# Rotary products by VectorE straight from the PSUM bank, sums by POOL, and one output addition moved up in an attention, LoRA and expert kernel

## The chip, the cores and the metric

The kernel runs on one core of a Trainium2 chip. The core has five engines with a queue of instructions each: TensorE (PE, matrix products into the eight PSUM banks), VectorE (DVE), ScalarE (ACT), GpSimd (POOL) and SyncE (SP, which issues DMAs). They run side by side and wait for each other through semaphores. The metric is the device time of one execution in microseconds, lower is better.

## The reference, cut to what matters

`x` has 64 batches of 64 tokens with 512 channels. The attention block is the part that the change touches:

```
h = cond(x) @ WA + bA;  kv_lat, q_lat = split(h)            # 2 x 128 latents per token
kRt = rope(h @ WB + bB);  qRt = rope(h @ WC + bC)            # one rotary key (64), 16 rotary queries (64 each)
rope(y) = y * cos + rot(y) * sin,   rot(y) = (-y1, y0, -y3, y2, ...)
scores = (q . k + qRt . kRt) * scale, causal;  attn = softmax(scores)
x = x + (attn @ v) @ WZ + bZ
x = x + ffn(cond2(x))                                        # LoRA product, then top-2 routing to 4 experts
```

`cos` and `sin` depend on the position and on the pair of features; both features of a pair have the same angle.

## The kernel before

Weights are first multiplied together (`absorb_weights`): the query weights into the key weights (`Ah`, `Al`), the value weights into WZ (`Mh`, `Ml`). An fp32 product is made of three matmuls on a high and a low part (`split_product`, L93). Then comes `attention`, then `routing`, then `experts`. `routing` and `experts` are not touched.

`attention` goes over 8 groups of 8 batches, so 512 token columns (GT) per group. Within a group there are 8 steps `i` (4 pairs of batches, times 2 halves of the 16 heads): scores, softmax, transpose of the probabilities, `mix` with the values, and `wz`, the output product of that step, which is accumulated in the single bank `bank_o` over eight heads and added to `x_res` by VectorE (`x2_tile`, L726). The next step's `wz` may not start before that addition (wait on `x2_ev`, L957).

The projections of a group are: one for the rotary keys (`rope_keys`, six matmuls into `bank_p1`), eight for the rotary queries (`q_rope_mm`, steps u = 0 to 7, two heads each, six matmuls), and 16 key heads (`keys_absorbed`, three matmuls). They share two banks, `bank_p0` and `bank_p1`: the query steps 0 to 3 use bank 0 and the key heads 0 to 3 bank 1; the key heads 4 and up, and the query steps 4 to 7, use the two by turns.

Every engine's order is written out by hand. TensorE's program at the boundary from group g to g+1 (L1031 to L1045) is: the first four heads of `wz` step 5, the rotary keys, then for u = 0 to 3 query step u, key head u and one more head of `wz` step 5; then the key heads 4 to 7, `wz` step 6 (whose first matmul waits for `x2_tile` of step 5), and the scores of g+1. In the middle of a group (L991 to L1002) the query steps 4 to 7 are interleaved with `wz` step 0, and after a transpose the key heads 8 and 9 follow, then `mix` and `wz` step 1 interleaved with the other key heads. In the first group, before the loop, the projections stand without output products between them.

What happens to a rotary projection before the change, with r counting keys and query steps:

- ScalarE (`keys_raw` L528, `q_raw` L534) copies the bank with its bias into `rope_raw` and raises `raw_ev`. This releases the bank: `q_rope_mm` and `keys_absorbed` on TensorE wait for `raw_ev` (L878, L886, L890, L892).
- POOL (`keys_cos` L447, `q_cos` L454) multiplies `rope_raw` by the cosine table into `k_rope` or `q_rope`.
- VectorE (`turn` L664) swaps neighbouring partitions of `rope_raw` with a shuffle, multiplies the result by the signed sine table, and adds it to POOL's product (`keys_rope` L677, `queries_rope` L685). This raises `rope_done`, for which the scores wait (L905).

VectorE's program at the boundary (L803 to L817) is: the low part of `mix` step 6, the rotary keys, the query steps 0 to 3, `x2_tile` step 5, `x2_tile` step 6, and the softmax of the next group. In the middle (L761 to L770): the query steps 4 and 5, a softmax sum, query step 6, `x2_tile` step 0, query step 7.

Of the kernel before, what the change touches and what calls it, by code (L numbers as in the profile page):

```python
# [63 lines left out]
def const_columns():  # L64
    def rope(feature, size):
        theta = np.exp(-(feature // 2).astype(np.float32) / np.float32(size)
                       * np.log(np.float32(10000.0))).astype(np.float32)
        angle = (np.arange(1, C + 1, dtype=np.float32)[None] * theta[:, None]).astype(np.float32)
        sign = np.where(feature % 2 == 0, -1.0, 1.0).astype(np.float32)[:, None]
        return np.cos(angle), np.sin(angle) * sign  # L70
# [264 lines left out]
def attention(nc, K, A, W, out):  # L335

    with ExitStack() as ctx:
# [6 lines left out]
        def sem(name):  # L344
# [15 lines left out]
        q_rope = sb("q_rope", [P, UB, GT])  # L360
        raw, swapped = sb("rope_raw", [P, 2, GT]), sb("rope_swapped", [P, GT])
        lat_bias = (raw[:, 0, :], swapped)
        bias_sel = nc.alloc_sbuf_tensor_at("bias_sel", [2 * LOW, GB, C], F32R, offset=nc.sbuf_base - GT * 4)
        score = sb("score", [P, HB, C])
# [13 lines left out]
        names = """xres_biased wrap_ev bias_sel_ready bias_mm lb_ev cond_mm cond_hi cond_lo lat_mm lat_ev lat_hi lat_lo  # L378
            kvt_mm kvt_ev keys_mm qr_mm raw_ev swap_ev cos_ev sin_ev rope_done ka_mm ka_ev s_mm score_ev max_ev sub_ev
            exp_ev sum_ev inv_ev prob_ev pt_mm pt_ev mix0_mm mix1_mm mix0_hi mix1_hi mix0_lo mix1_lo wz_mm x2_ev""".split()  # L380
# [58 lines left out]
        def _(pool):  # L439
# [6 lines left out]

            def keys_cos(g):  # L447
                pool.wait_ge(S["raw_ev"], g * NR + 1)
                nc.gpsimd.tensor_tensor(k_rope[:, :].rearrange("p (b t) -> p b t", b=GB),
                                        raw[:, 0, :].rearrange("p (b t) -> p b t", b=GB),  # L450
                                        K.parts["cosk"].unsqueeze(1).to_broadcast([P, GB, C]),
                                        ALU.mult).then_inc(S["cos_ev"], 1)

            def q_cos(g, u):  # L454
                pool.wait_ge(S["raw_ev"], g * NR + u + 2)
                cos = K.parts["cosq"][:, u * C:(u + 1) * C]
                nc.gpsimd.tensor_tensor(q_rope[:, u % UB, :].rearrange("p (b t) -> p b t", b=GB),  # L457
                                        raw[:, (u + 1) % 2, :].rearrange("p (b t) -> p b t", b=GB),
                                        cos.unsqueeze(1).to_broadcast([P, GB, C]), ALU.mult).then_inc(S["cos_ev"], 1)


# [11 lines left out]
            def project_front(g):  # L473
                keys_cos(g)
                for u in range(UB):
                    q_cos(g, u)

# [6 lines left out]
            def body(g, more):  # L484
                gated(g, 2)
                residual_bias(g, 0)
                for u in range(UB, NU):
                    q_cos(g, u)
                gated(g, 3)
# [17 lines left out]
        def _(act):  # L507
# [19 lines left out]

            def keys_raw(g):  # L528
                act.wait_ge(S["lat_ev"], g * 2 + 2)
                act.wait_ge(S["keys_mm"], g + 1)  # L530
                nc.scalar.activation(raw[:, 0, :], bank_p[1][:, :], ACT.Identity, bias=K["bB"][:, 0:1]
                                     ).then_inc(S["raw_ev"], 1)

            def q_raw(g, u):  # L534
                act.wait_ge(S["qr_mm"], g * NU + u + 1)
                if u:
                    act.wait_ge(S["swap_ev"], g * NR + u)
                    act.wait_ge(S["cos_ev"], g * NR + u)
                nc.scalar.activation(raw[:, (u + 1) % 2, :], bank_p[q_bank(u)][:, :], ACT.Identity, bias=K["bC"][:, u:u + 1]  # L539
                                     ).then_inc(S["raw_ev"], 1)  # L540

            def keys_absorbed(g, h):
# [19 lines left out]
            def first():  # L562
                latent_bias(0)
                for c in range(TC):
                    cond_hi(0, c)
                latent_hi(0, 0)
                latent_hi(0, 1)
                keys_raw(0)
                for u in range(UB):
                    q_raw(0, u)  # L570
                    keys_absorbed(0, u)
                for h in range(UB, HB):
                    keys_absorbed(0, h)
                exps(0, 0)
                kv_tokens(0, 0)
                kv_tokens(0, 1)
                exps(0, 1)

            def body(g, more):
# [5 lines left out]
                mix_hi(g, 1)  # L585
                q_raw(g, UB)
                exps(g, 3)
                for u in range(UB + 1, NU):
                    q_raw(g, u)

# [32 lines left out]
                if more:  # L623
                    keys_raw(g + 1)
                    for u in range(UB):
                        q_raw(g + 1, u)
                        keys_absorbed(g + 1, u)
# [14 lines left out]
        def _(dve):  # L642
# [20 lines left out]

            def turn(r, k, sin):  # L664

                dve.wait_ge(S["raw_ev"], r + 1)
                dve.wait_ge(S["rope_done"], r)
                nc.vector.memset(wait_here[:, :], 0.0)
                nc.vector.stream_shuffle(swapped[:, :], raw[:, k, :], [i ^ 1 for i in range(32)]
                                         ).then_inc(S["swap_ev"], 1)  # L670
                dve.wait_ge(S["swap_ev"], r + 1)
                v = swapped[:, :].rearrange("p (b t) -> p b t", b=GB)
                nc.vector.tensor_tensor(v, v, sin.unsqueeze(1).to_broadcast([P, GB, C]), ALU.mult
                                        ).then_inc(S["sin_ev"], 1)
                dve.wait_ge(S["sin_ev"], r + 1)

            def keys_rope(g):  # L677
                r = g * NR
                dve.wait_ge(S["lat_ev"], g * 2 + 2)
                turn(r, 0, K.parts["sink"])  # L680
                dve.wait_ge(S["cos_ev"], r + 1)
                nc.vector.tensor_tensor(k_rope[:, :], k_rope[:, :], swapped[:, :], ALU.add
                                        ).then_inc(S["rope_done"], 1)

            def queries_rope(g, u):  # L685
                r = g * NR + 1 + u
                turn(r, (u + 1) % 2, K.parts["sinq"][:, u * C:(u + 1) * C])
                dve.wait_ge(S["cos_ev"], r + 1)
                nc.vector.tensor_tensor(q_rope[:, u % UB, :], q_rope[:, u % UB, :], swapped[:, :], ALU.add
                                        ).then_inc(S["rope_done"], 1)  # L690

# [64 lines left out]
            def body(g, more):  # L756
# [1384 lines left out]
```

## Time and profile before

| | us |
|---|---|
| median of the two runs | 1875.18 (1873.96 to 1876.39) |
| the profiled execution, its time | 1876.52 |
| its span, first to last instruction | 1874.7 |
| TensorE busy | 1797.6 (96%) |
| VectorE busy | 925.5 (49%) |
| POOL busy | 702.7 (37%) |
| ScalarE busy | 630.2 (34%) |

Engines are PE, PEld (weight load of TensorE), DVE, ACT, POOL and SP. L12 is line 12 of the kernel. In a list of waits a row reads: who waited, at which tile and line, for whom; us in total, times, longest. In a timeline a row has the start and the duration in us, the engine, the line, the operation and its output and input tiles; in brackets stands the idle time before it and what ended it. Ends of matmuls are modelled, so that successive ones overlap: their spacing is the difference of their starts. PEclk is the granted TensorE clock as a share of full speed.

### The profile page before, as it was taken

What the parts mean: (1) busy time and instruction counts of PE and PEld (TensorE: products, weight loads), DVE (VectorE), ACT (ScalarE), POOL (GpSimd) and SP (SyncE); (2) the same over time, 40 slices, a digit from 0 to 9 for tenths busy, and PEclk for the clock granted to TensorE, in tenths of its full rate; (3) what the DMA queues carried; (4) which work ended last, traced back from release to release, by engine and by line L of the source; (5) the groups of instructions that cost most, each with busy time, mean ns of one, the idle gap of its engine ahead of it and who ended that gap; (6) DMA issues with size and microseconds to landing.
All of it is one profiled execution on the core that took longest, in us unless ns stands there. A gap on an engine that the chain in (4) does not pass through costs nothing. (4 is left out here: it accounts for less than half of the span.)

```text
span 1874.7 us, 29070 instructions
## 1 busy us (share of the span) xinstructions
PE 1797.6 (96%) x10656; PEld 1425.3 (76%) x10656; DVE 925.5 (49%) x1579; ACT 630.2 (34%) x1092; POOL 702.7 (37%) x526
## 2 busy tenths in 40 slices
PE   6799999999999999999999997999999999999997
PEld 4577777777777777777787776888888888888886
DVE  3565767566566656656423683242424233333332
ACT  4333333333333333333223112333333333333332
POOL 1231323123132312313000034565757575757564
PEclk9999999999999999999999998999999999999999
DMA  7000102010010102002123115033304230522011
GB/s 265 23 1 23 46 7 62 7 61 3 29 40 6 63 7 63 1 29 51 45 96 113 56 68 191 23 79 111 78 0 112 90 67 0 134 90 45 0 23 23
DMA packets 68795, 104.49 MB, mean 56 GB/s; under 512 B 12528, under 2 KB 29680, under 8 KB 68720
## 3 DMA queue, kind: packets, MB, share of 16 engines
q1 hardware_dynamic: 53568, 76.85, 12.3%
q0 software_dynamic: 7200, 16.78, 5.0%
q10 hardware_dynamic: 7952, 9.73, 1.4%
q8 instruction: 62, 1.02, 0.2%
q14 instruction: 13, 0.11, 0.0%
HBM read 78.18 MB, written 25.17 MB: 55 GB/s over the span
## 5 line engine op out<-in xcount | busy, mean ns | idle before, releaser
L1911 DVE CAST hh<-hid 128x512 fp32r<-128x512 f32 x128 | 95.5, 746 | 437.5 <-ACT hid L1838 437.5
L1754 POOL TENSOR_TENSOR w1l<-w_raw,w1h 128x512 fp32r<-128x512 f32 x112 | 185.0, 1652 | 146.7 <-ACT w1h L1830 146.6
L464 POOL TENSOR_TENSOR prob<-prob,rinv 128x512 f32<-128x512 f32 x64 | 66.7, 1043 | 436.2 <-DVE rinv L724 436.2
L97 PE MATMUL bank_o<-Mh,mix_h 128*128 128x512 f32 x512 | 210.2, 411 | 17.9 <-DVE x_res L731 16.5
L97 PE MATMUL e_h<-xh,w1h 128*128 (+1 forms) x512 | 201.0, 393 | 5.9 <-POOL w1l L1754 5.9
L99 PE MATMUL bank_o<-Mh,mix_l 128*128 128x512 f32 x512 | 203.6, 398 | 0.0
L98 PE MATMUL bank_o<-Ml,mix_h 128*128 128x512 f32 x512 | 203.5, 398 | 0.0
L97 PE MATMUL e_y<-w2h,hh 128*128 128x512 f32 x512 | 200.8, 392 | 1.5 <-DVE hl L1913 1.1
L98 PE MATMUL e_h<-xl,w1h 128*128 (+1 forms) x512 | 200.0, 391 | 0.0
L99 PE MATMUL e_h<-xh,w1l 128*128 (+1 forms) x512 | 200.0, 391 | 0.0
L99 PE MATMUL e_y<-w2h,hl 128*128 128x512 f32 x512 | 199.4, 389 | 0.0
L98 PE MATMUL e_y<-w2l,hh 128*128 128x512 f32 x512 | 199.2, 389 | 0.0
L1759 POOL TENSOR_TENSOR w2l<-w_raw,w2h 128x512 fp32r<-128x512 f32 x112 | 156.9, 1402 | 45.7 <-ACT w2h L1834 45.7
L1838 ACT ACTIVATE hid<-e_h 128x512 f32<-128x512 f32 x128 | 76.7, 599 | 245.4 <-PE e_h L99 245.4
L97 PEld LDWEIGHTS bank_o<-Mh,mix_h 128*128 128x128 f32 x512 | 98.3, 192 | 47.0 <-issue 25.7
L1834 ACT CAST w2h<-w_raw 128x512 fp32r<-128x512 f32 x112 | 69.7, 623 | 176.9 <-PE e_y L99 176.9
L457 POOL TENSOR_TENSOR q_rope<-rope_raw,table_attend 128x512 f32<-128x512 f32 x64 | 93.4, 1459 | 66.3 <-ACT rope_raw L539 66.2
L97 PEld LDWEIGHTS e_h<-xh,w1h 128*128 128x128 f32 x512 | 96.7, 189 | 26.6 <-POOL w1l L1754 6.8
L731 DVE TENSOR_TENSOR x_res<-bank_o,x_res 128x512 f32<-128x512 f32 x64 | 44.2, 691 | 145.4 <-PE bank_o L99 145.3
L99 PEld LDWEIGHTS bank_o<-Mh,mix_l 128*128 128x128 f32 x512 | 98.4, 192 | 22.0
L97 PEld LDWEIGHTS e_y<-w2h,hh 128*128 128x128 f32 x512 | 96.1, 188 | 24.1 <-DVE hl L1913 4.7
L98 PEld LDWEIGHTS bank_o<-Ml,mix_h 128*128 128x128 f32 x512 | 98.7, 193 | 18.9
(309 smaller groups left out, 3525.4 us busy)
## 6 DMA issues: line engine op xcount, KB each, us to landing
w_raw<-in_W_dram SPq DMA_DIRECT2D x56, 512.0 KB, 4.2
stage<-in_x_dram SPq DMA_DIRECT2D x8, 1024.0 KB, 6.0
x_res<-in_x_dram SPq DMA_DIRECT2D x32, 256.0 KB, 2.7
out_dram<-x_res SPq DMA_DIRECT2D x32, 256.0 KB, 2.0
flat_dram<-flat_sb ACTq DMA_DIRECT2D x32, 256.0 KB, 2.0
rows<-out_dram SPq DMA_DIRECT2D x4, 1024.0 KB, 5.3
stage<-in_W_dram SPq DMA_DIRECT2D x8, 512.0 KB, 5.2
x_res<-out_dram SPq DMA_DIRECT2D x3, 1024.0 KB, 5.1
```

Of the source, the lines that this page charges most:

```text
L97: nc.tensor.matmul(out, ah, bh, start=start and n == 0, stop=False)
L98: nc.tensor.matmul(out, ah, bl, start=False, stop=False)
L99: last = nc.tensor.matmul(out, al, bh, start=False, stop=stop and n == len(pairs) - 1)
L457: nc.gpsimd.tensor_tensor(q_rope[:, u % UB, :].rearrange("p (b t) -> p b t", b=GB), raw[:, (u + 1) % 2, :].rearrange("p (b t) -> p b t", b ...
L464: nc.gpsimd.tensor_tensor(prob[:, i % 2, :, :], prob[:, i % 2, :, :], rinv[:, :].unsqueeze(2).to_broadcast([P, HB, C]), ALU.mult).then_inc ...
L731: nc.vector.tensor_tensor(x_res[:, t, :], bank_o[:, :], x_res[:, t, :], ALU.add).then_inc(S["x2_ev"], 1)
L1754: nc.gpsimd.tensor_tensor(w1l[:, k, :, :], w1_at(pair, chunk), w1h[:, k, :, :].bitcast(F32), ALU.subtract).then_inc(S["w1_lo"], 1)
L1759: nc.gpsimd.tensor_tensor(w2l[:, k, :], w2_at(pair, chunk), w2h[:, k, :].bitcast(F32), ALU.subtract).then_inc(S["w2_lo"], 1)
L1834: nc.scalar.copy(w2h[:, k, :], w2_at(pair, chunk)).then_inc(S["w2_hi"], 1)
L1838: nc.scalar.activation(hid[:, slot, :], bank_h[k][:, :], ACT.Gelu).then_inc(S["h_act"], 1)
L1911: nc.vector.tensor_copy(hh[:, k, :], hid[:, k, :]).then_inc(S["h_hi"], 1)
```

## The change

The two products with cosine and sine are made by VectorE, each with one instruction that reads the bank, adds the bias and multiplies by the table; the first goes to `k_rope` or `q_rope`, the second to a buffer `rope_sin`, which is then shuffled into one of two `swapped` buffers. The sign of the sine table is changed accordingly, as the product now comes before the swap. POOL adds the two parts. ScalarE's copies and the tile `rope_raw` are gone; `raw_ev` is now raised by VectorE's second product. The waits of TensorE are as before. On VectorE's queue at the boundary, `x2_tile` of step 5 stands ahead of query step 3 instead of behind it.

```diff
-        sign = np.where(feature % 2 == 0, -1.0, 1.0).astype(np.float32)[:, None]
+        sign = np.where(feature % 2 == 0, 1.0, -1.0).astype(np.float32)[:, None]
...
-        raw, swapped = sb("rope_raw", [P, 2, GT]), sb("rope_swapped", [P, GT])
-        lat_bias = (raw[:, 0, :], swapped)
+        by_sin, swapped = sb("rope_sin", [P, GT]), sb("rope_swapped", [P, 2, GT])
+        lat_bias = (swapped[:, 0, :], swapped[:, 1, :])
...
-            def q_cos(g, u):
-                pool.wait_ge(S["raw_ev"], g * NR + u + 2)
-                cos = K.parts["cosq"][:, u * C:(u + 1) * C]
-                nc.gpsimd.tensor_tensor(q_rope[:, u % UB, :].rearrange("p (b t) -> p b t", b=GB),
-                                        raw[:, (u + 1) % 2, :].rearrange("p (b t) -> p b t", b=GB),
-                                        cos.unsqueeze(1).to_broadcast([P, GB, C]), ALU.mult).then_inc(S["cos_ev"], 1)
+            def q_sum(g, u):
+                pool.wait_ge(S["cos_ev"], g * NR + u + 2)
+                pool.wait_ge(S["swap_ev"], g * NR + u + 2)
+                nc.gpsimd.tensor_tensor(q_rope[:, u % UB, :], q_rope[:, u % UB, :], swapped[:, (u + 1) % 2, :], ALU.add
+                                        ).then_inc(S["rope_done"], 1)
...
-            def q_raw(g, u):
-                act.wait_ge(S["qr_mm"], g * NU + u + 1)
-                if u:
-                    act.wait_ge(S["swap_ev"], g * NR + u)
-                    act.wait_ge(S["cos_ev"], g * NR + u)
-                nc.scalar.activation(raw[:, (u + 1) % 2, :], bank_p[q_bank(u)][:, :], ACT.Identity, bias=K["bC"][:, u:u + 1]
-                                     ).then_inc(S["raw_ev"], 1)
...
-            def turn(r, k, sin):
+            def turn(g, k, out, rows, bias, cos, sin):
+                def by(out, table):
+                    return nc.vector.scalar_tensor_tensor(
+                        out=out.rearrange("p (b t) -> p b t", b=GB), in0=rows.rearrange("p (b t) -> p b t", b=GB),
+                        scalar=bias, in1=table.unsqueeze(1).to_broadcast([P, GB, C]), op0=ALU.add, op1=ALU.mult)
+                r = g * NR + k
+                by(out, cos).then_inc(S["cos_ev"], 1)
+                if k:
+                    dve.wait_ge(S["swap_ev"], r)
+                by(by_sin[:, :], sin).then_inc(S["raw_ev"], 1)
                 dve.wait_ge(S["raw_ev"], r + 1)
-                dve.wait_ge(S["rope_done"], r)
+                if k > 1:
+                    dve.wait_ge(S["rope_done"], r - 1)
                 nc.vector.memset(wait_here[:, :], 0.0)
-                nc.vector.stream_shuffle(swapped[:, :], raw[:, k, :], [i ^ 1 for i in range(32)]
+                nc.vector.stream_shuffle(swapped[:, k % 2, :], by_sin[:, :], [i ^ 1 for i in range(32)]
                                          ).then_inc(S["swap_ev"], 1)
-                dve.wait_ge(S["swap_ev"], r + 1)
-                v = swapped[:, :].rearrange("p (b t) -> p b t", b=GB)
-                nc.vector.tensor_tensor(v, v, sin.unsqueeze(1).to_broadcast([P, GB, C]), ALU.mult
-                                        ).then_inc(S["sin_ev"], 1)
-                dve.wait_ge(S["sin_ev"], r + 1)
...
             def queries_rope(g, u):
-                r = g * NR + 1 + u
-                turn(r, (u + 1) % 2, K.parts["sinq"][:, u * C:(u + 1) * C])
-                dve.wait_ge(S["cos_ev"], r + 1)
-                nc.vector.tensor_tensor(q_rope[:, u % UB, :], q_rope[:, u % UB, :], swapped[:, :], ALU.add
-                                        ).then_inc(S["rope_done"], 1)
+                cols = slice(u * C, (u + 1) * C)
+                dve.wait_ge(S["qr_mm"], g * NU + u + 1)
+                turn(g, u + 1, q_rope[:, u % UB, :], bank_p[q_bank(u)][:, :], K["bC"][:, u:u + 1],
+                     K.parts["cosq"][:, cols], K.parts["sinq"][:, cols])
...
                 mix_lo(g, 6)
                 if more:
                     keys_rope(g + 1)
-                    for u in range(UB):
+                    for u in range(3):
                         queries_rope(g + 1, u)
                 x2_tile(g, 5)
+                if more:
+                    for u in range(3, UB):
+                        queries_rope(g + 1, u)
                 x2_tile(g, 6)
```

## Rows read from the trace of the kernel before

**Rows 1.** The page's engines: busy us, share of the span, instructions.

```profile
PE 1797.6 (96%) x10656; PEld 1425.3 (76%) x10656; DVE 925.5 (49%) x1579; ACT 630.2 (34%) x1092; POOL 702.7 (37%) x526
```

**Rows 2.** Waits of TensorE in the attention stage: us in total, times, longest.

```profile
PE bank_o L97 <- DVE x_res L731: 16.5, 9, 2.2
```

**Rows 3.** Windows, two successive groups: length, busy us by engine, PEclk, DMA share, GB/s.

```profile
175.20:284.20 109.00, 106.39 (x776) 82.28 (x775) 69.57 (x127) 38.94 (x68) 28.21 (x22) 0.98 0.09 30
284.20:391.60 107.40, 104.80 (x777) 81.14 (x775) 69.56 (x127) 38.94 (x68) 28.14 (x22) 1.00 0.10 30
```

**Rows 4.** Windows behind a boundary stall and behind a pause of 1.38 us.

```profile
179.40:182.80 3.40, 3.40 (x10) 2.68 (x9) 0.00 (x0) 0.00 (x0) 0.00 (x0) 0.53 0.26 82
926.80:930.20 3.40, 3.40 (x17) 2.82 (x16) 0.00 (x0) 0.00 (x0) 0.00 (x0) 1.00 0.00 0
```

**Rows 5.** Timeline of the boundary from the second group to the third.

```profile
267.43 1.28 DVE L695 TENSOR_TENSOR mix_l<-bank_m,mix_h 128x512 fp32r<-128x512 f32 x2
...
270.31 0.39 PE L99 MATMUL bank_p<-lat_h,WBl 128*128 128x512 f32 x1
...
273.26 0.39 PE L97 MATMUL bank_p<-lat_h,WCh 128*128 128x512 f32 x1
...
274.39 0.39 PE L99 MATMUL bank_p<-lat_h,WCl 128*128 128x512 f32 x1
...
280.32 0.69 DVE L689 TENSOR_TENSOR q_rope<-q_rope,rope_swapped 128x512 f32<-128x512 f32 x1
...
281.18 0.76 DVE L669 STREAM_SHUFFLE rope_swapped<-rope_raw 128x512 f32<-128x512 f32 x1
...
281.42 0.39 PE L97 MATMUL bank_p<-lat_h,Ah 128*128 128x512 f32 x1
...
284.20 0.40 PE L99 MATMUL bank_p<-lat_h,Al 128*128 128x512 f32 x1
...
286.00 0.68 DVE L731 TENSOR_TENSOR x_res<-bank_o,x_res 128x512 f32<-128x512 f32 x1
286.83 0.47 PE L97 MATMUL bank_o<-Mh,mix_h 128*128 128x512 f32 x1 [2.23 <-DVE x_res L731]
```

**Rows 6.** Single lines: count, ns shortest/median/longest, first and last start, shapes.

```profile
L673 DVE TENSOR_TENSOR rope_swapped<-rope_swapped,table_attend x72: 691/1024/1510, 67.6 to 868.4; 128x512 f32<-128x512 f32 x72
L707 DVE SCALAR_TENSOR_TENSOR score<-bank_s,table_attend x64: 650/692/693, 82.2 to 901.9; 128x512 f32<-128x512 f32 x64
L1928 DVE TENSOR_SCALAR y_sb<-e_y,slot_gate x14: 741/746/751, 1241.6 to 1778.5; 128x512 f32<-128x512 f32 x14
L470 POOL TENSOR_TENSOR x_res<-x_res,bZ x32: 1259/1514/1754, 94.9 to 886.1; 128x512 f32<-128x512 f32 x32
```

**Rows 7.** Timeline of the middle of the third group.

```profile
320.62 0.69 ACT L539 ACTIVATE rope_raw<-bank_p,bC 128x512 f32<-128x512 f32 x1 [2.03 <-DVE rope_swapped L669]
...
321.42 0.39 PE L99 MATMUL bank_o<-Mh,mix_l 128*128 128x512 f32 x1
...
321.92 0.69 DVE L731 TENSOR_TENSOR x_res<-bank_o,x_res 128x512 f32<-128x512 f32 x1
...
322.79 0.40 PE L97 MATMUL bank_p<-lat_h,Ah 128*128 128x512 f32 x1
```

**Rows 8.** Timeline of the first group's projections.

```profile
65.47 0.39 PE L99 MATMUL bank_p<-lat_h,WBl 128*128 128x512 f32 x1
...
67.28 0.69 ACT L539 ACTIVATE rope_raw<-bank_p,bC 128x512 f32<-128x512 f32 x1 [0.64 <-PE bank_p L99]
...
68.02 0.50 PE L97 MATMUL bank_p<-lat_h,WCh 128*128 128x512 f32 x1
...
75.32 0.50 PE L97 MATMUL bank_p<-lat_h,Ah 128*128 128x512 f32 x1
...
77.96 1.28 ACT L544 COPY k_absorbed<-bank_p 128x512 f32<-128x512 f32 x2 [0.36 <-PE bank_p L99]
...
80.40 1.08 PE L912 MATMUL bank_s<-k_absorbed,q 128*64 128x256 f32 x8 [1.79 <-DVE q_rope L689]
```

More of the change, by code:

```diff
@@ L360, in attention @@
         q_rope = sb("q_rope", [P, UB, GT])
-        raw, swapped = sb("rope_raw", [P, 2, GT]), sb("rope_swapped", [P, GT])
-        lat_bias = (raw[:, 0, :], swapped)
-        bias_sel = nc.alloc_sbuf_tensor_at("bias_sel", [2 * LOW, GB, C], F32R, offset=nc.sbuf_base - GT * 4)
+        by_sin, swapped = sb("rope_sin", [P, GT]), sb("rope_swapped", [P, 2, GT])
+        lat_bias = (swapped[:, 0, :], swapped[:, 1, :])
+        bias_sel = nc.alloc_sbuf_tensor_at("bias_sel", [2 * LOW, GB, C], F32R, offset=nc.sbuf_base - 3 * GT * 4)
         score = sb("score", [P, HB, C])
@@ L378, in attention @@
         names = """xres_biased wrap_ev bias_sel_ready bias_mm lb_ev cond_mm cond_hi cond_lo lat_mm lat_ev lat_hi lat_lo
-            kvt_mm kvt_ev keys_mm qr_mm raw_ev swap_ev cos_ev sin_ev rope_done ka_mm ka_ev s_mm score_ev max_ev sub_ev
+            kvt_mm kvt_ev keys_mm qr_mm raw_ev swap_ev cos_ev rope_done ka_mm ka_ev s_mm score_ev max_ev sub_ev
             exp_ev sum_ev inv_ev prob_ev pt_mm pt_ev mix0_mm mix1_mm mix0_hi mix1_hi mix0_lo mix1_lo wz_mm x2_ev""".split()
@@ L445, in bias_rows, with keys_sum @@
                                         ALU.mult).then_inc(S["bias_sel_ready"], 1)
[L447 to L452, printed above, removed]
-            def q_cos(g, u):
-                pool.wait_ge(S["raw_ev"], g * NR + u + 2)
-                cos = K.parts["cosq"][:, u * C:(u + 1) * C]
-                nc.gpsimd.tensor_tensor(q_rope[:, u % UB, :].rearrange("p (b t) -> p b t", b=GB),
-                                        raw[:, (u + 1) % 2, :].rearrange("p (b t) -> p b t", b=GB),
-                                        cos.unsqueeze(1).to_broadcast([P, GB, C]), ALU.mult).then_inc(S["cos_ev"], 1)
+            def keys_sum(g):
+                pool.wait_ge(S["cos_ev"], g * NR + 1)
+                pool.wait_ge(S["swap_ev"], g * NR + 1)
+                nc.gpsimd.tensor_tensor(k_rope[:, :], k_rope[:, :], swapped[:, 0, :], ALU.add
+                                        ).then_inc(S["rope_done"], 1)
[3 more added lines that the diff above has]
+                nc.gpsimd.tensor_tensor(q_rope[:, u % UB, :], q_rope[:, u % UB, :], swapped[:, (u + 1) % 2, :], ALU.add
+                                        ).then_inc(S["rope_done"], 1)
             def gated(g, i):
@@ L473, in project_front @@
             def project_front(g):
-                keys_cos(g)
+                keys_sum(g)
                 for u in range(UB):
-                    q_cos(g, u)
+                    q_sum(g, u)
             def first():
@@ L487, in body @@
                 for u in range(UB, NU):
-                    q_cos(g, u)
+                    q_sum(g, u)
                 gated(g, 3)
@@ L526, in kv_tokens @@
                                ).then_inc(S["kvt_ev"], 1)
[L528 to L531, printed above, removed]
-                                     ).then_inc(S["raw_ev"], 1)
-            def q_raw(g, u):
-                act.wait_ge(S["qr_mm"], g * NU + u + 1)
-                if u:
-                    act.wait_ge(S["swap_ev"], g * NR + u)
-                    act.wait_ge(S["cos_ev"], g * NR + u)
-                nc.scalar.activation(raw[:, (u + 1) % 2, :], bank_p[q_bank(u)][:, :], ACT.Identity, bias=K["bC"][:, u:u + 1]
-                                     ).then_inc(S["raw_ev"], 1)
             def keys_absorbed(g, h):
@@ L567, in first @@
                 latent_hi(0, 1)
-                keys_raw(0)
                 for u in range(UB):
-                    q_raw(0, u)
                     keys_absorbed(0, u)
@@ L585, in body @@
                 mix_hi(g, 1)
-                q_raw(g, UB)
                 exps(g, 3)
-                for u in range(UB + 1, NU):
-                    q_raw(g, u)
                 prob_transposed(g, 2)
@@ L623, in body @@
                 if more:
-                    keys_raw(g + 1)
                     for u in range(UB):
-                        q_raw(g + 1, u)
                         keys_absorbed(g + 1, u)
@@ L672, in turn @@
-                v = swapped[:, :].rearrange("p (b t) -> p b t", b=GB)
-                nc.vector.tensor_tensor(v, v, sin.unsqueeze(1).to_broadcast([P, GB, C]), ALU.mult
-                                        ).then_inc(S["sin_ev"], 1)
-                dve.wait_ge(S["sin_ev"], r + 1)
             def keys_rope(g):
-                r = g * NR
                 dve.wait_ge(S["lat_ev"], g * 2 + 2)
-                turn(r, 0, K.parts["sink"])
-                dve.wait_ge(S["cos_ev"], r + 1)
-                nc.vector.tensor_tensor(k_rope[:, :], k_rope[:, :], swapped[:, :], ALU.add
-                                        ).then_inc(S["rope_done"], 1)
+                dve.wait_ge(S["keys_mm"], g + 1)
@@ L685, in queries_rope @@
+                turn(g, 0, k_rope[:, :], bank_p[1][:, :], K["bB"][:, 0:1], K.parts["cosk"], K.parts["sink"])
             def queries_rope(g, u):
-                r = g * NR + 1 + u
-                turn(r, (u + 1) % 2, K.parts["sinq"][:, u * C:(u + 1) * C])
-                dve.wait_ge(S["cos_ev"], r + 1)
-                nc.vector.tensor_tensor(q_rope[:, u % UB, :], q_rope[:, u % UB, :], swapped[:, :], ALU.add
-                                        ).then_inc(S["rope_done"], 1)
+                cols = slice(u * C, (u + 1) * C)
```

## The prediction

> **What bounds the kernel now.** I read the page's table of engines first: TensorE is busy for 96% of the span, VectorE for 49%, POOL for 37% [rows 1]. A microsecond taken from VectorE, POOL or ScalarE is worth something only where TensorE stands still for it. So the second view is the list of waits, for TensorE alone, over the attention stage. One entry stands out: 16.5 us for L731, the output addition [rows 2]. Seven of its nine waits are 2.23 us long and recur once per group, at the boundary where the next group's projections run; the other two are 0.44 us in the last group.
>
> The third view, windows cut from boundary to boundary, shows a second part of the same loss: one group takes 107.40 us, the one before it 109.00 [rows 3]. Of the seven stalls of 2.23 us six are followed, within four microseconds, by some eight matmuls at twice their spacing; in that stretch the granted clock is 0.53, the lower of its two levels (1.2 against 2.4 GHz) [rows 4]. The group of 107.40 us has no such stretch. So the boundary costs 7 x 2.3 us of idle time and 6 x 1.6 us of clock, some 26 us of 1875. That is all that a better boundary could give back. A pause of 1.38 us near 924 us is followed by a stretch at full clock [rows 4].
>
> The timeline of one boundary gives the cause [rows 5]. TensorE interleaves, per query step, six matmuls into bank_p0, three for a key head and three of the sixth output step; these steps are 2.72 us apart (three from 273.26 to 281.42). VectorE runs three operations for the keys and for each query step and only then, at 286.00, the output addition; TensorE has issued the last key head at 284.20 and waits until 286.83.
>
> **What the change removes.** ScalarE loses nine copies per group (0.69 us, as the one in rows 7). ScalarE is idle around them, so that gains nothing by itself; the copies had a second job, though: each released the PSUM bank 0.69 us after it was filled. VectorE still has three operations per step (two products, one shuffle; before, a shuffle, a product, a sum). What goes is their slow form: the product from SBUF took 0.69 us at best, 1.02 in the median and 1.51 at most [rows 6], while POOL was running. An operation that reads PSUM and one table is steady: L707, the same instruction type, takes 0.65 to 0.69 [rows 6]. The Trainium skill, page "SBUF — State Buffer", section "SBUF: two separate sides", says why: VectorE with two SBUF inputs and POOL exclude each other for a whole instruction. The trace agrees (0.69 against 1.51), and by that rule alone the chain of VectorE would end earlier and the stall go; that is the third rival below.
>
> **What it adds: the bank is held for two products.** Prices, all from rows. A reader starts 0.50 us after the start of the last matmul (321.42 to 321.92) [rows 7]. A pair of VectorE operations from PSUM takes 1.28 [rows 5], I take 1.29; TensorE follows 0.05 us after a release (67.28 + 0.69 to 68.02), and its first matmul then takes 0.50 instead of 0.39, so 0.11 more [rows 8]. The shuffle follows its operand after 0.17 us (280.32 + 0.69 to 281.18) and takes 0.76 [rows 5]; the next operation may start 0.10 before its end, the overlap in the pair. A matmul's place is 0.227 us (five from 273.26 to 274.39 [rows 5]).
>
> The new instruction, with a bias per partition, is not in the trace. Below: L707 at its fastest, a pair of 1.25. Above: L1928, from PSUM with a factor per partition, 0.75 each [rows 6], a pair of 1.41. I take 1.29, since L1928 also fetches an address from a register, which the new one doesn't.
>
> *The boundary*, with the times of [rows 5]:
> - Keys: last matmul 270.31, products 270.81 to 272.10, so the first key head starts at 272.15; its place was 270.31 + 7 x 0.227 = 271.90. TensorE is 0.25 + 0.11 = 0.36 behind.
> - First query step: its bank is full at 270.31 + 6 x 0.227 + 0.50 = 272.17, but VectorE shuffles the keys until 272.93; products end 274.22. The second step starts at 274.27; its place was 273.26 + 0.36 = 273.62. Behind: 0.36 + 0.65 + 0.11 = 1.12.
> - Second step: last matmul 274.39 + 1.12 = 275.51, products 276.01 to 277.30, third step 277.35; its place was 273.26 + 2.72 + 1.12 = 277.10. Behind: 1.48. The third costs the same: 1.84.
> - Then the moved addition. It stands on VectorE's queue ahead of the fourth step's products and waits for the sixth output step, whose last matmul is the one before the fifth key head: 281.42 - 0.23 + 1.84 = 283.03. Addition from 283.53, products 284.13 to 285.42. The fifth key head needs the bank that they read (L890): it starts at 285.47, and its place was 283.26. Behind: 1.84 + 2.21 + 0.11 = 4.16.
> - The seventh output step now finds its addition done; it starts at 284.20 + 0.23 + 4.16 = 288.59. Before, it started at 286.83, with a first matmul 0.08 longer (0.47): 286.91. So 1.7 us are lost per boundary, seven times: 11.8. The stall of 2.23 has only moved from behind the key heads to ahead of the last four.
>
> *The middle of a group* [rows 7]. Steps five to eight use two banks by turns, which hides the longer hold. Only the eighth is exposed: VectorE runs the first output addition before it (as before), at 321.92; then products 322.52 to 323.81. The tenth key head needs their bank (L892). It started at 322.79, since ScalarE had copied the bank from 320.62; now 323.86. Lost: 1.07 + 0.11 = 1.18, in eight groups 9.4.
>
> *The first projections* [rows 8], with no output step between: keys' last matmul 65.47, products to 67.26, shuffle, products of the first step 68.09 to 69.38, second step 69.43. Each further one takes 0.11 + 5 x 0.227 + 0.50 + 1.29 + 0.05 = 3.09: 72.52, 75.61, fifth key head 78.70 instead of 75.32. The last key copy ends 3.38 later than 77.96 + 1.28, at 82.62; the scores start at 82.67 instead of 80.40: 2.3.
>
> *POOL and the rest cost nothing.* The sums on POOL (1.26 at best, 1.51 in the median, L470 [rows 6]) come after the shuffles, the last of a boundary by 288; the scores that need it follow the seventh output step, 24 matmuls or 5.4 us behind the key heads. In the middle the division by the row sums queues behind the eighth sum, some 3 us later than now; its transpose is issued behind an output step and six key heads, 42 matmuls or 9.5 us. Without that cover each would cost TensorE about 1.5 us per group. The moved addition starts its output DMA 2.5 us sooner; nothing waits for that.
>
> A second page speaks against the change: the Trainium skill, "VectorE: DVE Perf Modes", "Rules for kernel authors", advises to copy PSUM to SBUF first when many operations use a matmul's output. The rows show no slower operation from PSUM (0.69 both ways); what they charge is the bank held 1.29 instead of 0.69.
>
> **Sum.** 11.8 + 9.4 + 2.3 = 23.5 us. With pairs of 1.25: 21.6; of 1.41: 0.60 more per boundary, 0.12 per middle, 0.60 at the start, 29.3. For the clock I take no difference: a pause as long as today's stays in each boundary (2.21 against 2.23), and those of the middle (1.07) are shorter than the one of 1.38 that left the clock up. The profiled execution took 1876.5 us (span 1874.7); the two runs shown have a median 1.3 lower. 1876.5 + 23.5 = 1900.0; against the median 1898.7. I say 1900.
>
> **The rivals.**
> - *The clock also falls at the middle pauses.* With 1.2 to 1.3 us of idle time it may: eight times 1.6 us, 13 more, 1913. For it: 2.23 was enough six times in seven. Against it: 1.38 was not [rows 4].
> - *The clock stops falling at the boundary*, since the idle time is spread over five pauses: 9.7 less, 1890. For it: one boundary in seven went without. Against: the largest pause hasn't shrunk.
> - *Not slower.* VectorE, free of POOL, releases every bank before TensorE returns to it, and the addition no longer holds up the seventh output step: 7 x 2.3 of idle time and 9.7 of clock go, 1849. This is what the skill's rule on the shared ports would bring. The point that decides is whether the fourth step's products end before TensorE reaches the fifth key head (283.26 above). Against it: the addition ahead of them can't start before 283.53, in whatever time the products run.
>
> **Chances.** Forecast 0.64, clock in the middle 0.17, clock kept at the boundary 0.12, not slower 0.07. The range from 1888 to 1914 holds the first and third and about half of the second; the forecast's own, by the pairs, is 1897 to 1906. Two per cent, about what a measurement of this kernel can tell from no change, is 37.5 us: slower by over that needs 1912.7 or more, half of the second case and a tail of the first, 0.14. Faster by over 2% would need more than the whole boundary returned: 0.02. Within: 0.84.
>
> **What would show it.** In the list of waits, TensorE's waits for L731 vanish from the boundaries, and waits for VectorE's second product appear: per group one of about 2.2 us ahead of the fifth key head, one of 1.1 ahead of the tenth, and three to four of 0.2 to 0.7. From boundary to boundary a group takes 109.0 + 1.7 + 1.2 = 111.9 us. The products take 0.69 with POOL busy or not. It is wrong if the fifth key head starts without a wait, if the products take over 0.75, or if a stretch at the lower clock follows the tenth key head.

## The result and the profile after

The changed kernel takes 1898.21 us, the median of two runs (1897.07 to 1899.35), against 1875.18 before: a ratio of 1.0125, 95% interval 1.0101 to 1.0150. It is 23 us slower. The profiled execution took 1899.35 us; its span is 1897.5.

The page's table of engines answers [rows 1]. TensorE has about the same work, and every other engine has less: VectorE 36 us, ScalarE 48, POOL 18. None of that shortened the span, which is 22.8 us longer than before (1897.5 against 1874.7).

```profile
PE 1804.0 (95%) x10656; PEld 1420.3 (75%) x10656; DVE 889.6 (47%) x1579; ACT 582.5 (31%) x1020; POOL 684.6 (36%) x526
```

The waits of TensorE in the attention stage of the changed kernel (who waited, for whom, us in total, times, longest) answer [rows 2]:

```profile
PE bank_p L97 <- DVE rope_sin L643: 29.5, 27, 2.1
...
PE bank_o L97 <- DVE x_res L709: 0.9, 2, 0.4
```

L709 is the output addition, L731 before: of its nine waits only the two short ones of the last group are left. In their place stand 27 waits for VectorE's second product, which releases the bank of a key or query step. The timeline sorts them: seven of 2.10 us ahead of a group's fifth key head, eight of 1.03 ahead of the tenth, seven of 0.41 ahead of the second query step, and five, 3.8 us together, in the first projections (14.7 + 8.2 + 2.9 + 3.8 = 29.6, the 29.5 of the list but for rounding).

Windows from the fifth key head of one group to that of the next (length, then busy us of TensorE, weight load, VectorE, ScalarE and POOL, PEclk, DMA share, GB/s), as [rows 3], and behind three of the pauses, as [rows 4]:

```profile
180.20:292.20 112.00, 107.67 (x775) 81.89 (x775) 64.94 (x127) 33.01 (x58) 25.85 (x22) 0.98 0.09 29
292.20:402.80 110.60, 106.27 (x775) 80.75 (x775) 64.93 (x127) 33.01 (x58) 25.86 (x22) 1.00 0.09 29
403.40:406.80 3.40, 3.40 (x9) 2.61 (x8) 0.18 (x1) 1.31 (x3) 1.28 (x1) 0.50 0.22 69
292.30:295.70 3.40, 3.40 (x14) 2.42 (x15) 0.69 (x2) 1.84 (x4) 1.29 (x1) 1.00 0.37 110
332.60:336.00 3.40, 3.40 (x18) 2.35 (x19) 1.44 (x3) 1.66 (x3) 2.61 (x3) 1.00 0.00 0
```

A group at full clock takes 110.60 us where it took 107.40, so 3.2 more. The third and fourth window stand behind two pauses of 2.10 us: one was followed by the lower level of the clock (0.50), the other was not. In this execution the clock fell behind five of the seven, before behind six of seven. The last window stands behind a pause of 1.03 us in the middle of a group: full clock.

The boundary from the second group to the third, timeline of the changed kernel (start, duration, engine, line, operation; in brackets the idle time before it and what ended it; here and in the timelines below, the rows of other instructions are left out), answers [rows 5]:

```profile
276.84 0.39 PE L99 MATMUL bank_p<-lat_h,WBl 128*128 128x512 f32 x1
...
277.27 0.75 DVE L643 SCALAR_TENSOR_TENSOR k_rope<-bank_p,bias,table_attend 128x512 f32<-128x512 f32 x1 [2.03 <-PE bank_p L99]
277.94 0.74 DVE L643 SCALAR_TENSOR_TENSOR rope_sin<-bank_p,bias,table_attend 128x512 f32<-128x512 f32 x1
278.73 0.50 PE L97 MATMUL bank_p<-lat_h,Ah 128*128 128x512 f32 x1
278.73 0.72 DVE L656 STREAM_SHUFFLE rope_swapped<-rope_sin 128x512 f32<-128x512 f32 x1
279.35 0.73 DVE L643 SCALAR_TENSOR_TENSOR q_rope<-bank_p,bC,table_attend 128x512 f32<-128x512 f32 x1
...
280.80 0.49 PE L97 MATMUL bank_p<-lat_h,WCh 128*128 128x512 f32 x1 [0.41 <-DVE rope_sin L643]
...
283.95 0.50 PE L97 MATMUL bank_p<-lat_h,WCh 128*128 128x512 f32 x1
...
289.78 0.39 PE L99 MATMUL bank_o<-Mh,mix_l 128*128 128x512 f32 x1
...
290.20 0.69 DVE L709 TENSOR_TENSOR x_res<-bank_o,x_res 128x512 f32<-128x512 f32 x1 [2.38 <-PE bank_o L99]
290.81 0.74 DVE L643 SCALAR_TENSOR_TENSOR q_rope<-bank_p,bC,table_attend 128x512 f32<-128x512 f32 x1
291.47 0.74 DVE L643 SCALAR_TENSOR_TENSOR rope_sin<-bank_p,bC,table_attend 128x512 f32<-128x512 f32 x1
292.27 0.50 PE L97 MATMUL bank_p<-lat_h,Ah 128*128 128x512 f32 x1 [2.10 <-DVE rope_sin L643]
...
295.42 0.39 PE L97 MATMUL bank_o<-Mh,mix_h 128*128 128x512 f32 x1
```

The last six rows are the new stall. The addition waits for the sixth output step, whose last matmul starts at 289.78; the fourth query step's products, whose bank has long been full, stand behind it on VectorE's queue; TensorE is idle for 2.10 us until they release the bank. The seventh output step, for which the addition was moved up, then starts without a wait.

The pause of 1.03 us in the middle of the third group answers [rows 7]. The addition and the eighth query step's two products run one after the other, and the tenth key head waits for the second product:

```profile
330.45 0.69 DVE L709 TENSOR_TENSOR x_res<-bank_o,x_res 128x512 f32<-128x512 f32 x1 [0.40 <-PE bank_o L99]
...
331.06 0.74 DVE L643 SCALAR_TENSOR_TENSOR q_rope<-bank_p,bC,table_attend 128x512 f32<-128x512 f32 x1
...
331.72 0.74 DVE L643 SCALAR_TENSOR_TENSOR rope_sin<-bank_p,bC,table_attend 128x512 f32<-128x512 f32 x1
...
332.52 0.51 PE L97 MATMUL bank_p<-lat_h,Ah 128*128 128x512 f32 x1 [1.03 <-DVE rope_sin L643]
```

The first projections, from the keys' last matmul to the first scores, answer [rows 8]:

```profile
65.21 0.39 PE L99 MATMUL bank_p<-lat_h,WBl 128*128 128x512 f32 x1
...
81.38 1.28 ACT L527 COPY k_absorbed<-bank_p 128x512 f32<-128x512 f32 x2 [0.37 <-PE bank_p L99]
...
82.72 1.08 PE L893 MATMUL bank_s<-k_absorbed,q 128*64 128x256 f32 x8 [0.68 <-ACT k_absorbed L527]
```

### The profile page after: what moved, and what is told of

It is laid out like the page before. It is cut to its first block and busy times, and to the rows that moved or that the text cites. A ratio compares the mean times of both kernels' runs of the same rounds, so it can differ in the third digit from the quotient of the medians.

```text
span 1897.5 us, 28870 instructions
## 1 busy us (share of the span) xinstructions
PE 1804.0 (95%) x10656; PEld 1420.3 (75%) x10656; DVE 889.6 (47%) x1579; ACT 582.5 (31%) x1020; POOL 684.6 (36%) x526
## 5 line engine op out<-in xcount | busy, mean ns | idle before, releaser
L97 PE MATMUL bank_o<-Mh,mix_h 128*128 128x512 f32 x512 | 206.2, 403 | 2.3 <-DVE mix_l L673 1.4
L527 ACT COPY k_absorbed<-bank_p 128x512 f32<-128x512 f32 x128 | 75.1, 587 | 189.1 <-PE bank_p L99 187.5
L456 POOL TENSOR_TENSOR q_rope<-q_rope,rope_swapped 128x512 f32<-128x512 f32 x64 | 82.3, 1286 | 131.2 <-DVE rope_swapped L656 131.2
L709 DVE TENSOR_TENSOR x_res<-bank_o,x_res 128x512 f32<-128x512 f32 x64 | 44.2, 691 | 178.5 <-PE bank_o L99 176.1
```

The costliest lines, as they stand in the source:

```text
L97: nc.tensor.matmul(out, ah, bh, start=start and n == 0, stop=False)
L456: nc.gpsimd.tensor_tensor(q_rope[:, u % UB, :], q_rope[:, u % UB, :], swapped[:, (u + 1) % 2, :], ALU.add).then_inc(S["rope_done"], 1)
L527: nc.scalar.copy(kabs[:, h % HB, :], bank_p[key_bank(h)][:, :]).then_inc(S["ka_ev"], 1)
L709: nc.vector.tensor_tensor(x_res[:, t, :], bank_o[:, :], x_res[:, t, :], ALU.add).then_inc(S["x2_ev"], 1)
```

## The experiments

All are timed against the kernel before, which took 1875.37 us beside the first, second, third and fifth of them and 1876.38 beside the fourth and the sixth.

**The moved addition put back.** The changed kernel, with the addition of the sixth step behind all four query steps again:

```diff
-                    for u in range(3):
+                    for u in range(UB):
                         queries_rope(g + 1, u)
                 x2_tile(g, 5)
-                if more:
-                    for u in range(3, UB):
-                        queries_rope(g + 1, u)
```

> The changed kernel with one thing undone: the output addition of the sixth step stands behind query step 3 again. Theory (the bank of the fourth query step is held until the addition ahead of it has run): the wait of 2.10 us ahead of the fifth key head shrinks to about 0.25 and the addition still ends before the seventh output step needs it, since VectorE's step is now 2.2 us against TensorE's 2.7. Per boundary 2.0 us less, seven times 13.7, so 1884.5 us; if the fall of the clock hangs on the long pause, 7 us less again, 1877. Rival (two products per bank are too long wherever the addition stands): no change, 1898. Rival (the early addition is a help): the wait of 2.2 us comes back ahead of the seventh output step, 1898 or more.

It took 1877.84 us (1874.92 to 1880.43), ratio 1.0012 (1.0003 to 1.0021). TensorE's waits for the second product, and a group, in this kernel:

```profile
PE bank_p L97 <- DVE rope_sin L643: 14.9, 20, 1.1
```

```profile
273.70:382.30 108.60, 106.23 (x776) 80.73 (x775) 64.96 (x126) 33.01 (x58) 25.88 (x22) 1.00 0.09 30
```

The seven waits of 2.10 us are gone (27 to 20, 29.5 to 14.9), a group is 2.0 us shorter, and no stretch at the lower clock is left at the boundaries. So the moved line costs the changed kernel 20.4 us (1898.2 - 1877.8): 7 x 2.0 of order, and the rest is about what the five falls of the clock cost. The addition needed no earlier place here: behind the four query steps it still starts at 287.79, while TensorE runs the last four key heads (from 287.17), and the seventh output step starts at 290.31 without a wait:

```profile
287.79 0.67 DVE L709 TENSOR_TENSOR x_res<-bank_o,x_res 128x512 f32<-128x512 f32 x1
...
290.31 0.40 PE L97 MATMUL bank_o<-Mh,mix_h 128*128 128x512 f32 x1
```

**The same move alone.** The kernel before, with nothing but the addition one place sooner:

```diff
-                    for u in range(UB):
+                    for u in range(3):
                         queries_rope(g + 1, u)
                 x2_tile(g, 5)
+                if more:
+                    for u in range(3, UB):
+                        queries_rope(g + 1, u)
```

> The kernel before with the move alone: the output addition of the sixth step ahead of query step 3, rotary work as before (ScalarE's copies release the banks). Theory: the seven waits of 2.23 us and their restarts go (16.1 us) and with them the stretches at the lower clock (9.7 us): 1849 us; with the clock still falling, 1859. Rival (the early addition is a loss by itself, as it holds up the fourth query step): the scores or a key head wait instead, 1875 or more.

1849.41 us (1848.06 to 1849.84), ratio 0.9857 (0.9842 to 0.9872): faster than both kernels. A group, and VectorE and TensorE at the boundary, in this kernel:

```profile
267.10:372.20 105.10, 104.72 (x776) 81.14 (x775) 69.46 (x126) 38.95 (x67) 28.14 (x22) 1.00 0.10 31
```

```profile
278.78 1.05 DVE L673 TENSOR_TENSOR rope_swapped<-rope_swapped,table_attend 128x512 f32<-128x512 f32 x1
279.86 0.69 DVE L689 TENSOR_TENSOR q_rope<-q_rope,rope_swapped 128x512 f32<-128x512 f32 x1
...
280.47 0.68 DVE L731 TENSOR_TENSOR x_res<-bank_o,x_res 128x512 f32<-128x512 f32 x1
...
281.02 0.40 PE L99 MATMUL bank_p<-lat_h,Al 128*128 128x512 f32 x1
281.08 0.73 DVE L669 STREAM_SHUFFLE rope_swapped<-rope_raw 128x512 f32<-128x512 f32 x1
281.30 0.47 PE L97 MATMUL bank_o<-Mh,mix_h 128*128 128x512 f32 x1
```

The last key head and the seventh output step follow each other almost at TensorE's own spacing (0.28 against 0.23), and the group is 2.3 us shorter than the 107.40 of [rows 3]. The products still have their slow form (1.05 us here), and no matmul of the boundary waits for it. One line, moved by one place, is worth -26.0 us where ScalarE's copy releases the bank, and +20.4 us where the release stands behind the moved line.

**The first addition of a group put later.** The changed kernel, with the addition ahead of the eighth query step behind it:

```diff
-                x2_tile(g, 0)
                 queries_rope(g, 7)
+                x2_tile(g, 0)
```

> The changed kernel with the first output addition behind the eighth query step instead of ahead of it. Theory: the tenth key head no longer waits (1.03 us and 0.11 for the restart), eight groups, 9.1 us less: 1889.1. The addition ends about 0.8 us later, some 1.2 us before the next output step asks for it. Rival (the next output step then waits for the addition instead): no gain, 1898. Rival (the wait there is for POOL's sums, not for the bank): no change.

1883.27 us (1880.98 to 1884.42), ratio 1.0039 (1.0025 to 1.0052). The list of waits, and a group, in this kernel:

```profile
PE bank_p L97 <- DVE rope_sin L643: 21.3, 19, 2.1
```

```profile
290.70:400.20 109.50, 106.20 (x776) 80.76 (x776) 64.83 (x126) 33.00 (x58) 25.88 (x23) 1.00 0.09 30
289.10:292.50 3.40, 3.40 (x14) 2.43 (x15) 0.63 (x1) 1.90 (x4) 1.29 (x1) 1.00 0.35 103
```

The eight waits of 1.03 us are gone, and a group is 1.1 us shorter (110.60 to 109.50), as expected. The kernel gained 6 us more than that, about what five falls of the clock cost. The seven pauses of 2.10 us are all still there, but in this profile none is followed by the lower clock; the second window stands behind one of them. One more profile of this kernel (the next text calls it that of the second experiment) and one of the changed kernel show whether that holds.

> The same kernel as in the second experiment, profiled once more, for the clock alone. There seven pauses of 2.10 us were followed by no stretch at the lower clock, in the changed kernel five of seven were. Theory (whether the clock falls behind a pause of that length depends on when it falls, not on the kernel): some of the seven fall now, each for about 1.3 us; span 1881.5 plus that. Rival (without the pause in the middle of a group the clock holds): none again, span 1881.5 within 2 us.

> The changed kernel itself, profiled once more, for the clock alone. Theory (chance in when the pause falls): another number than five of seven stretches at the lower clock. Rival (a property of the kernel): five again, or six.

The kernel of this experiment took 1883.54 us in that further execution, with two falls in seven pauses of 2.10 us; the changed kernel took 1897.50, with four in seven. Two stretches of the former, behind two pauses of the same length in the same execution:

```profile
179.90:183.30 3.40, 3.40 (x8) 2.71 (x9) 0.65 (x1) 1.09 (x2) 1.27 (x1) 0.51 0.32 104
290.60:294.00 3.40, 3.40 (x14) 2.43 (x15) 0.72 (x2) 1.83 (x4) 1.29 (x1) 1.00 0.34 112
```

The number of falls differs between executions of one kernel (five and four; none and two). Nine in fourteen against two in fourteen hints that it also depends on what the rest of the group does.

That the two executions of this kernel, with none and with two falls, are only 0.3 us apart has its cause in another fall. From the first pause of 2.10 us to the last, the one with two falls takes 2.45 us more (659.36 against 656.91). Behind a pause of 1.89 us at the start of `routing` it is the other one that runs at the lower clock, and it takes 3.3 us more from there to TensorE's next wait (18.93 against 15.60). The stretch behind that pause, first in the execution without falls at the boundaries, then in the one with two:

```profile
940.40:943.80 3.40, 3.40 (x17) 3.40 (x18) 1.45 (x3) 1.76 (x3) 0.00 (x0) 0.52 0.79 223
```

```profile
943.15:946.55 3.40, 3.40 (x32) 3.40 (x32) 2.11 (x4) 2.73 (x6) 0.00 (x0) 1.00 0.68 234
```

The profiled executions of the kernel before and of the changed one both have that fall (18.92 us each), so that it does not enter their difference. What decides whether such a pause is followed by the lower clock stays open.

**Both additions late.** The edits of the first and the third experiment together, so that no addition stands ahead of a product that releases a bank for which TensorE waits.

> Both edits at once: in the changed kernel the sixth step's addition stands behind query step 3 again, and the first step's addition behind the eighth query step. Theory (the two waits for a bank are independent of each other): the gain of the second adds to the first, 8 x 1.14 = 9.1 us: 1877.8 - 9.1 = 1868.7, that is 6.7 us faster than the kernel before. Rival (the idle time only moves on, since VectorE has no slack left): 1877.

1868.08 us (1867.89 to 1870.83), ratio 0.9960 (0.9947 to 0.9974). A group, and the waits, in this kernel:

```profile
272.70:380.20 107.50, 106.18 (x776) 80.79 (x776) 64.79 (x126) 33.01 (x58) 25.86 (x22) 1.00 0.09 30
```

```profile
PE bank_p L97 <- DVE rope_sin L643: 6.6, 12, 1.1
```

This is the new rotary step with nothing in its way. Against the move alone, where ScalarE's copies release the banks, a group is 2.4 us longer (107.50 against 105.10); with the first projections (2.6, counted from the keys' last matmul) that makes 7 x 2.4 + 2.6 = 19.4, where the medians differ by 18.7. That is the price of holding each bank for two products instead of one copy.

**Copies kept, the rest as changed.** The sums stay on POOL, the two products on VectorE, the addition at its early place; but ScalarE copies each bank to SBUF as before, and both products read the copy (part of the edit against the changed kernel):

```diff
+                nc.scalar.activation(raw[:, (u + 1) % 2, :], bank_p[q_bank(u)][:, :], ACT.Identity, bias=K["bC"][:, u:u + 1]
+                                     ).then_inc(S["raw_ev"], 1)
...
-                    return nc.vector.scalar_tensor_tensor(
-                        out=out.rearrange("p (b t) -> p b t", b=GB), in0=rows.rearrange("p (b t) -> p b t", b=GB),
-                        scalar=bias, in1=table.unsqueeze(1).to_broadcast([P, GB, C]), op0=ALU.add, op1=ALU.mult)
+                    return nc.vector.tensor_tensor(
+                        out.rearrange("p (b t) -> p b t", b=GB), raw[:, k, :].rearrange("p (b t) -> p b t", b=GB),
+                        table.unsqueeze(1).to_broadcast([P, GB, C]), ALU.mult)
```

> The same division of work as in the changed kernel (both products by VectorE, shuffle, sum by POOL) and the same early addition, but the products read ScalarE's copy in SBUF, as copied before the change, so that a bank is released after one copy of 0.69 us. The sine product is made in place and there is one shuffle buffer. Theory (what costs is the hold of the bank): no key head waits, though VectorE's products are slowed by POOL's sums to 1.0 to 1.5 us each; the addition ends near the time at which the seventh output step asks for it: about 1851 us. Rival (what costs is that VectorE makes both products, or POOL the sums): VectorE's chain is the longest of all here, so 1898 or more.

1851.71 us (1850.52 to 1852.52), ratio 0.9869 (0.9854 to 0.9885). A group of this kernel, one of its products, and the POOL sum beside that one:

```profile
269.50:374.40 104.90, 104.52 (x776) 81.18 (x776) 72.92 (x126) 38.98 (x67) 26.89 (x22) 1.00 0.10 31
```

```profile
276.13 1.57 POOL L456 TENSOR_TENSOR q_rope<-q_rope,rope_swapped 128x512 f32<-128x512 f32 x1 [1.47 <-DVE rope_swapped L675]
...
276.59 1.66 DVE L664 TENSOR_TENSOR rope_raw<-rope_raw,table_attend 128x512 f32<-128x512 f32 x1
```

VectorE is busier here than in any other of these kernels (72.92 us per group against 64.94 in the changed one), its product from SBUF took 1.66 us beside a POOL sum instead of the 0.69 that is its median, and still a group is 5.7 us shorter than in the changed kernel (110.60). So neither the sums on POOL nor VectorE's busy time set the time; who releases the bank does. Against the move alone it gains nothing; it is 2.3 us slower, and 1.7 of that is the first wait of the scores for the rotated queries (3.5 us against 1.8). Behind that wait this profile also has a stretch at the lower clock (0.50 from 85.0 to 89.0), where the move alone is at full clock (1.00 from 83.4 to 87.4).

The Trainium skill, page "SBUF — State Buffer", section "SBUF: two separate sides", has it that VectorE with two SBUF inputs and GpSimd reading SBUF lock each other out for a whole instruction. The 1.66 us agree with that, and so do the steady products from PSUM in the changed kernel (below). Here the rule tells the durations, and not the kernel's time.

**The bias taken out.** The changed kernel with the scalar of both products a constant zero, which leaves the rotary biases out of the result:

```diff
-                        scalar=bias, in1=table.unsqueeze(1).to_broadcast([P, GB, C]), op0=ALU.add, op1=ALU.mult)
+                        scalar=0.0, in1=table.unsqueeze(1).to_broadcast([P, GB, C]), op0=ALU.add, op1=ALU.mult)
```

> The changed kernel with the constant zero in place of the bias per partition, so that the rotary biases are left out; all else the same. In the changed kernel a product takes 0.74 us and a pair 1.40, against 0.69 and 1.28 for operations without a scalar per partition. Theory (reading the bias costs 0.05 us per product): products 0.69, pairs 1.29; each bank is released 0.11 us sooner, five times per boundary, once per middle, five times at the start, in all 0.11 x (35 + 8 + 5) = 5.3 us less: 1892.9. Rival (the layout of 8 x 64 with the table repeated costs it): products 0.74, 1898.

1888.94 us (1885.93 to 1891.35), ratio 1.0063 (1.0049 to 1.0076). The second product with a bias (the changed kernel) and without (this one): count, shortest, median and longest in ns, first and last start, shape:

```profile
L643 DVE SCALAR_TENSOR_TENSOR rope_sin<-bank_p,bC,table_attend x64: 733/741/743, 68.5 to 889.9; 128x512 f32<-128x512 f32 x64
```

```profile
L643 DVE SCALAR_TENSOR_TENSOR rope_sin<-bank_p,table_attend x72: 669/680/683, 67.5 to 882.3; 128x512 f32<-128x512 f32 x72
```

A bias per partition costs each product 0.06 us. A pair without it takes 1.29 us, the value that the prediction had taken, with it 1.41. A group at full clock takes 109.76 us instead of 110.60:

```profile
221.49:331.25 109.76, 106.16 (x775) 80.75 (x776) 63.92 (x128) 33.03 (x58) 25.86 (x22) 1.00 0.09 30
```

Over eight groups and the first projections the bias is worth some 7 us. The rest of the 9.3 us between the medians is about what the clock gives: three falls in this profile, five in the changed kernel's.

## Why the prediction held, and where its steps were off

Set one above the other, the kernels make a staircase: 1849.4 with the addition early and the copies kept; 18.7 more where the bank is held for two products; 9.8 more with a group's first addition ahead of the eighth step (1877.8 against 1868.1); 20.4 more with the moved addition ahead of the fourth. The kernel before had lost 26.0 at another place of the same boundary, so the change comes to 18.7 + 9.8 + 20.4 - 26.0 = 22.9, where 23.0 was measured. The steps are differences of successive medians and add up by construction; what they show is the size of each.

**The mechanism.** The stall moved from behind the key heads to ahead of the last four, as said. The steps of the boundary, in us from the start of the keys' last matmul, as predicted (270.31 of [rows 5]) and in the timeline above (276.84):

| | predicted | measured |
|---|---|---|
| keys' products begin | 0.50 | 0.43 |
| first key head | 1.84 | 1.89 |
| first step's products begin | 2.62 | 2.51 |
| second step's matmuls | 3.96 | 3.96 |
| third step's matmuls | 7.04 | 7.11 |
| the addition | 13.22 | 13.36 |
| fifth key head | 15.16 | 15.43 |
| seventh output step | 18.28 | 18.58 |

Before, the last row was 16.52, or 16.60 with the slower first matmul; so a boundary lost 1.98 us where 1.68 was forecast. The third and fourth query step show no wait of TensorE: the modelled ends of its matmuls cover it, and the loss is in the spacing (0.51 from the last output matmul at 283.44 to 283.95, where 0.23 is the rule). The forecast of three to four small waits per boundary was therefore wrong as to the list of waits, which has one.

**The middle.** The wait ahead of the tenth key head is 1.03 us, forecast 1.07, in every one of the eight groups. 3.20 - 1.98 = 1.22 per group, forecast 1.18. That POOL's later division would cost nothing held: it starts at 334.61, and TensorE's waits for POOL in the attention stage come to 1.7 us in both kernels.

**The first projections.** The scores start at 82.72 instead of 80.40 [rows 8]. Counted from the keys' last matmul (65.21 and 65.47) that is 2.6 us later, where 2.3 was forecast. It is for another reason than in the kernel before: they wait for ScalarE's last key copy now, as the prediction had worked out, and no longer for a sum of VectorE.

**The prices.** The pair of products was the term that was too small: taken at 1.29 us from the nearer-looking L707 of [rows 6], measured 1.41, its upper bound, which came from L1928. The prediction had set that row aside since it fetches an address from a register; what the two share is the factor per partition, and the last experiment shows that this is what costs. The prediction's sign of being wrong, over 0.75, is just met by the keys' first product (0.751 to 0.752); the queries' take 0.74. With 1.41 in all its steps the prediction's own sum was 29.3. Two gaps were too large: the shuffle follows its operand after 0.05 us, not 0.17, and at the boundaries an idle VectorE starts its products 0.42 to 0.44 us after the last matmul's start, not 0.50. The kernel without the bias, whose pair has the predicted 1.29, shows what these gaps are worth: a group of 109.76 is 2.4 us above 107.40, where the prediction's boundary and middle add up to 2.9. Outside the clock the loss is 7 x 1.98 + 8 x 1.22 + 2.6 (the first projections, counted from the keys' last matmul) = 26.2, where 23.5 was said.

**The clock.** The step "no difference" failed in size: 6 falls of 1.6 us became 5 of 1.3, 3.1 us less, though the pause ahead of the fall had hardly shrunk (2.23 to 2.10). So two errors, 2.7 too little and 3.1 too much, nearly cancelled: 23.5 forecast, 23.0 measured. That is luck, as neither follows from the other. The same luck is in the forecast of 111.9 us for a group: it takes 111.9 to 112.0 with a fall, from a larger loss and a cheaper fall, and 110.6 without. As to the rivals: the clock did not fall at the middle pauses in any of these profiles. It did stop falling at all boundaries in one, so that the second rival, an execution near 1890 us, names something that happens, if not in the runs of the changed kernel. The third fell as the prediction had it, on the place of the addition and not on the products' speed; its price, 1849, is what the move alone reached.

## What to carry to other kernels

A copy that an idle engine makes is not waste if it is what releases a PSUM bank: before such a copy is taken out, count how long the bank is then held, and how many instructions of the new reader's queue stand ahead of the release. An early place in an in-order queue is only free for what waits behind the moved instruction if nothing behind it frees what the producer needs; the same move changed the time by -26 and by +20 us here. Price a fused operation by the row that shares its operands (here the scalar per partition), not by the one that shares its name.

The Trainium skill, page "VectorE: DVE Perf Modes", section "Rules for kernel authors", advises to copy PSUM to SBUF first when many operations use a matmul's output. Here two are already enough (1851.7 us with the copies, 1898.2 without, and still 1868.1 without them when both additions are out of the way), and for the bank's sake: the operation itself takes 0.68 us from PSUM without a bias and 0.69 from SBUF with POOL quiet.

## What the runs showed of the hardware that was not expected

- A scalar per partition instead of a constant lengthens a product of 128x512 from PSUM from 0.68 to 0.74 us.
- A pause of TensorE of 2.10 us is followed by a stretch at about half clock in some cases and not in others: in five and four of seven in two executions of the changed kernel, in none and two of seven in two executions of a kernel with the same pauses. In none of the profiles was one of 1.03 or 1.38 us followed by such a stretch. The length alone does not decide: the pause of 2.23 us ahead of the first projections was followed by full clock in all ten profiles, the one of 1.89 us at the start of `routing` by the lower level in six of the ten.
